# Self attention of a fused decoder layer: v as the weight in four column strips, sums taken from the exponentials, and a new order of the steps around them

## The reference, cut to what matters

```python
def _L0_attn_ref(x, Wq, Wk, Wv, Wo):            # H=32 heads, HKV=8 groups of G=4, DH=16
    q = (x @ Wq.T).reshape(b, t, H, DH).transpose(0, 2, 1, 3)
    k = (x @ Wk.T).reshape(b, t, HKV, DH).transpose(0, 2, 1, 3)
    v = (x @ Wv.T).reshape(b, t, HKV, DH).transpose(0, 2, 1, 3)
    q, k = rope(q), rope(k)
    scores = jnp.einsum('bhgtd,bhkd->bhgtk', q.reshape(b, HKV, G, t, DH), k) / math.sqrt(DH)
    scores = jnp.where(causal, scores, jnp.finfo(jnp.float32).min)
    attn = jax.nn.softmax(scores, axis=-1)
    ctx = jnp.einsum('bhgtk,bhkd->bhgtd', attn, v)
    return ctx.reshape(b, H, t, DH).transpose(0, 2, 1, 3).reshape(b, t, E) @ Wo.T

x = _layernorm(x + attn(x)); x = _layernorm(x + cross(x, ctx)); x = _layernorm(x + ffn(x))
```

## Time and profile before

| | |
|---|---|
| median of 3 runs | 1139.7 us (1138.28 to 1140.21) |
| profiled execution | 1137.65 us |
| its span, first to last instruction | 1135.9 us |
| mean granted clock of PE | 0.992 of full |
| busy: PE, PEld, DVE, ACT, POOL | 97%, 86%, 47%, 48%, 20% |
| chain that ended last | PE 90%, DVE 3%, ACT 3% |
| self attention, with the first cross projections | about 0 to 231 us of the span |
| cross attention, 16 groups | about 231 to 1076 us |

### The profile page before, as it was taken

How to read it: one execution, slowest core, us unless ns; L and a number is a source line. 1 busy time by engine, 2 the same in 40 slices (tenths; PEclk the granted TensorE clock), 3 DMA queues, 4 the chain that set the end, 5 groups by cost and what they waited for, 6 DMA issues and landing times.

```text
span 1135.9 us, 20112 instructions
## 1 busy us (share of the span) xinstructions
PE 1103.6 (97%) x6892; PEld 980.8 (86%) x6892; DVE 535.6 (47%) x2002; ACT 541.2 (48%) x1336; POOL 223.5 (20%) x235
## 2 busy tenths in 40 slices
PE   6899998999999999999999999999999999999897
PEld 5899998878888888888888888888888888888785
DVE  4577767544434343434243435344343444343584
ACT  5778776444444443444443443444444435344412
POOL 6335444321010101111010101010101011110142
PEclk9899998999999999999999999999999999999999
DMA  4401100132011010102020202021110101000001
GB/s 145 158 11 28 32 2 1 29 140 80 28 52 60 18 60 18 60 18 76 3 78 0 78 0 78 0 78 31 47 60 18 60 18 60 18 23 1 1 1 74
DMA packets 16600, 49.63 MB, mean 44 GB/s; under 512 B 2480, under 2 KB 4912, under 8 KB 16048
## 3 DMA queue, kind: packets, MB, share of 16 engines
q1 hardware_dynamic: 16272, 44.93, 11.6%
q0 software_dynamic: 288, 4.19, 0.9%
HBM read 47.02 MB, written 2.10 MB: 43 GB/s over the span
## 4 chain that ended last, share of the span: by engine, by line
PE 90%; DVE 3%; ACT 3%; issue 1%; DMA 1%; POOL 1%; SPq 0%; POOLq 0%; DVEq 0%; ACTq 0%
PE bank L650 49%; PE bank L1396 15%; PE bank L1383 5%; PE bank L1366 5%; PE bank L499 4%; PE bank L585 4%; PE bank L1414 3%; PE bank L1373 2%; PE bank L573 1%; PE bank L1320 1%; DMA v_raw<-in_wv 1%; PE bank L1452 1%; DMA stage<-in_wq 1%; DVE sm L429 1%; PE bank L509 0%
## 5 line engine op out<-in xcount | busy, mean ns | idle before, releaser
L810 POOL TENSOR_TENSOR bm<-mask,bias 128x512 f32<-128x512 f32 x64 | 96.9, 1515 | 715.6 <-DVE nmx L1090 460.9
L922 ACT ACTIVATE pr<-sm,nmx 128x128 f32<-128x128 f32 x256 | 99.8, 391 | 162.7 <-DVE nmx L1090 162.5
L1102 DVE TENSOR_TENSOR at_lo<-bank,at_hi 128x512 fp32r<-128x512 f32 x64 | 44.3, 692 | 252.8 <-ACT at_hi L936 252.8
L1108 DVE TENSOR_TENSOR acc<-acc,bank 128x512 f32<-128x512 f32 x128 | 87.8, 687 | 120.3 <-PE bank L1396 120.3
L915 ACT COPY v<-bank 128x256 f32<-128x256 f32 x124 | 46.2, 373 | 118.9 <-PE bank L650 67.7
L1396 PE MATMUL bank<-wo_hi,at_hi 128*128 128x512 f32 x256 | 101.2, 395 | 0.0
L1396 PE MATMUL bank<-wo_lo,at_hi 128*128 128x512 f32 x256 | 100.6, 393 | 0.0
L1396 PE MATMUL bank<-wo_hi,at_lo 128*128 128x512 f32 x256 | 99.9, 390 | 0.0
L650 PE MATMUL bank<-wv_hi,cT_hi 128*128 128x256 f32 x512 | 92.0, 302 | 0.0
L650 PE MATMUL bank<-wv_hi,cT_lo 128*128 128x256 f32 x512 | 81.9, 282 | 0.0
L650 PE MATMUL bank<-wv_lo,cT_hi 128*128 128x256 f32 x512 | 81.9, 282 | 0.0
(11 more groups left out here) (210 smaller groups left out, 2300.8 us busy)
## 6 DMA issues: line engine op xcount, KB each, us to landing
qk_raw<-in_wqk SPq DMA_DIRECT2D x31, 512.0 KB, 4.4
o_raw<-in_wo SPq DMA_DIRECT2D x16, 512.0 KB, 3.3
v_raw<-in_wv SPq DMA_DIRECT2D x15, 512.0 KB, 4.3
xT_raw<-in_xT SPq DMA_DIRECT2D x8, 256.0 KB, 2.7
acc<-in_x POOLq DMA_DIRECT2D x1, 2048.0 KB, 9.3
stage<-in_cT POOLq DMA_DIRECT2D x1, 2048.0 KB, 13.4
bias<-in_bias SPq DMA_DIRECT2D x16, 128.0 KB, 3.0
out<-acc SPq DMA_DIRECT2D x8, 256.0 KB, 2.0
```

The lines of the kernel that those rows point to most:

```text
L810: nc.gpsimd.tensor_tensor(bm[:, s % 2], mask[:, HALF * (s // HG):HALF * (s // HG + 1), :], bias[:, s % HG:s % HG + 1, :].broadcast_to([P, ...
L922: e = nc.scalar.activation(pr[:, s % 2, k], sm[:, s % 2, k], ACT.Exp, bias=nmx[:, s % 2, k:k + 1], accum_out=sums[:, s % 2, k:k + 1])
L1102: nc.vector.tensor_tensor(at[1][:, s // HG, s % HG], PO[:], f32(at[0][:, s // HG, s % HG]), ALU.subtract).then_inc(s_al, 1)
L1108: nc.vector.tensor_tensor(acc[:, b], acc[:, b], PX[b % 2][:], ALU.add).then_inc(s_acc, 1)
```

## The change

**v is the weight.** `pv(b, odd)` runs twice per element, for the even groups (0, 2, 4, 6) and the odd ones (1, 3, 5, 7). Its weight is 32 columns of a padded v (`v1` holds pairs of groups with zeros between them), its moving operand the 512 columns of a transposed tile of four heads, its output one of four strips of 32 partitions of one bank. The even products start the sums, the odd ones add to them. The output is already transposed, in another order of its rows; Wo is laid out in that order on the host. The tiles are worked through in the order of `GROUPS`. Five buffers (`RING`) hold transposed tiles, two of the old ones and three in `stage`.

**Sums from the exponentials.** Odd tiles sum by `accum_out` of ACT's exponentials, even tiles by a `tensor_reduce` of DVE. DVE takes one reciprocal per element, of the 32 sums widened to 512 columns. Four PE transposes (`spread`) turn it, ACT copies it to `y`, and DVE multiplies the output bank by it.

**Other moves in the self attention.** The widened copy of q goes from ACT to POOL, one step earlier; the rotation's sum and the turn of q one step earlier; the addition of x with its statistics, the layer norm's steps and the xn transposes move to other steps; the Wo product is cut in two halves (j=6 and j=7); the Wo weight is split by POOL and, in four pieces, DVE; part of the first k stack is copied by DVE; k and v of element 3 are projected at t=2, j=6.

**Between the stages.** The context comes in two halves of 1 MB: the first by POOL at t=2, j=7, the second by SP once the first is split, behind the second half of the first q and k weights, which now goes into `qk_raw[0]` once that is split. The high parts of the first cross weights are made by POOL and one element earlier. The first cross tiles have another order; one k product goes to a bank of scores (S[1]).

**Last group.** The last transposed copy (ACT) comes before the last exponentials; the first output product before the transposes of x; the low part of the last attention output before `norm_x`.

```diff
-            self.on = left(first, "on", [P, H1, DH1])
+            self.on = left(first, "on", [P, D])
-            self.v1 = left(first, "v1", [P, 4, G1, DH1 + 1])
+            self.v1 = left(first, "v1", [P, 4, G1 // 2, 3 * DH1])
...
+    GROUPS = (0, 2, 4, 6, 1, 3, 5, 7)
...
# POOL
-            if j == (3 if t == 1 else 5) and live(t):
+            if j == (3 if t == 1 else 4) and live(t):
                 ...   rot = rot_a + rot_b
+            if j == 5 and live(t):
+                nc.gpsimd.tensor_copy(q3[:, :, 0:2 * DH1]..., rot[:, 0:D]...broadcast_to([P, H1, 2, DH1])).then_inc(s_hi3, 1)
+            if j == 3 and t == 2:
+                nc.gpsimd.tensor_copy(wout[0][:], wout_raw).then_inc(s_wohi, 1)
-            if j == 6 and t == 2:
+            if j == 7 and t == 2:
                 nc.gpsimd.dma_start(acc[:], a["x"]).then_inc(s_res, 16)
-                nc.gpsimd.dma_start(stage[:], a["cT"]).then_inc(s_stage, 16)
+                nc.gpsimd.dma_start(mem.cT_raw, mem.context_half(a["cT"], 0)).then_inc(s_stage, 16)
# ACT
                     act.wait_ge(s_neg, n // 2 + 1)
+                    at_least(act, s_rs, b - 1)
                     for r in range(R1):
-                        e = nc.scalar.activation(pr[:, 1, r], sm[:, 1, r], ACT.Exp, bias=nmx[:, r:r + 1])
+                        e = nc.scalar.activation(pr[:, 1, r], sm[:, 1, r], ACT.Exp, bias=nmx[:, r:r + 1],
+                                                 accum_out=sums1[b % 2][:, GROUPS[i], r:r + 1])
...
-                at_least(act, s_pv, n - 1)
-                nc.scalar.copy(prT[:, i % 2], ...).then_inc(s_ptc, 1)
+                if n >= RING:
+                    act.wait_ge(s_pv, (n - RING) // 4 + 1)
+                nc.scalar.copy(prT[n % RING], pt_bank[i % 2][:]).then_inc(s_ptc, 1)
...
+            if j == 3 and live(t - 3):
+                b = t - 3
+                act.wait_ge(s_R, b + 1)
+                at_least(act, s_x1, b)
+                nc.scalar.copy(y[:], O1[:]).then_inc(s_Rc, 1)
# DVE
-        def normalise(b, i):
-            nc.vector.reciprocal(rs[:, hs], o[:, :, DH1]).then_inc(s_rs, 1)
-            nc.vector.tensor_tensor(on[:, hs, :], o[:, :, 0:DH1], rs[:, hs]..., ALU.mult).then_inc(s_on, 1)
-            if j == 1 and live(t - 4):
+            if j == 2 and live(t - 4):
                 ...   x1, xn
+            if j == 2 and live(t - 3):
+                b = t - 3
+                dve.wait_ge(s_p, G1 * (b + 1))
+                dve.wait_ge(s_sum, G1 // 2 * (b + 1))
+                at_least(dve, s_R, b)
+                nc.vector.reciprocal(rs, sums1[b % 2].rearrange("p g (r one) -> p r g one", one=1)
+                                     .broadcast_to([P, R1, G1, DH1])).then_inc(s_rs, 1)
+            if j == 4 and live(t - 3):
+                b = t - 3
+                dve.wait_ge(s_Rc, b + 1)
+                dve.wait_ge(s_pv, 2 * (b + 1))
+                at_least(dve, s_onlo, b)
+                nc.vector.tensor_tensor(on[:], O0[:], y[:], ALU.mult).then_inc(s_on, 1)
+            b, i, n = tile(t, j, 1)
+            if live(b) and i % 2 == 0:
+                dve.wait_ge(s_p, n + 1)
+                at_least(dve, s_rs, b - 1)
+                nc.vector.tensor_reduce(sums1[b % 2][:, GROUPS[i], :], pr[:, 0], AX_X, ALU.add).then_inc(s_sum, 1)
# PE
-        def pv(b, i, n):
-            pe.wait_ge(s_ptc, n + 1)
-            for r in range(R1):
-                ins = nc.tensor.matmul(o_bank[h // HB][:, col:col + DH1 + 1], prT[:, i % 2, r],
-                                       v1[:, b % 4, i, :], start=True, stop=True)
+        def pv(b, odd):
+            n = b * G1 + 4 * odd
+            pe.wait_ge(s_ptc, n + 4)
+            for k in range(4):
+                ins = nc.tensor.matmul(O0[4 * k * 8:4 * (k + 1) * 8, :], v1[:, b % 4, k, odd * DH1:(odd + 2) * DH1],
+                                       prT[(n + k) % RING], start=not odd, stop=bool(odd))
+            ins.then_inc(s_pv, 1)
+        def spread(b):
+            pe.wait_ge(s_rs, b + 1)
+            at_least(pe, s_Rc, b)
+            for r in range(R1):
+                ins = nc.tensor.transpose(O1[:, r * T:(r + 1) * T], rs[:, r].rearrange("p g d -> p (g d)"), ident[:])
+            ins.then_inc(s_R, 1)
-            b, i, n = tile(t, j, 3)
-            if live(b):
-                pv(b, i, n)
+            if j == 3 and live(t - 3):
+                spread(t - 3)
+                pv(t - 3, 1)
+            if j == 6 and live(t - 2):
+                pv(t - 2, 0)
# the first cross weights: DVE, t = LAST - 2, and POOL
+                    if t == LAST - 2 and j == 3:
+                        first_lo(wqk[0], qk_raw[0][:], s_wqk_h[0], s_wqk[0])
+                    if t == LAST - 2 and j == 0:
+                        first_hi(wqk[0], qk_raw[0][:], s_qk_in[0], s_wqk_h[0])
# PE, after t = LAST - 1
             step_a(LAST, 0)
             first_project_v(3)
             step_a(LAST, 1)
-            step_a(LAST, 2)
+            step_a(LAST, 3)
+            step_a(LAST, 4)
             groups(pe, step)
# last group: ACT, PE
+                    if last and s == TILES - 1:
+                        copy_prT(n - 1, False)
                     exps(n, s, first)
...
-                    transpose_x2(0)
-                    transpose_x2(1)
                     for j in range(HALF):
                         output(HALF + j, 1, n if j == 0 else None)
+                        if j == 0:
+                            transpose_x2(0)
+                            transpose_x2(1)
```

More of the change, by code:

```diff
@@ L103, in __init__ @@
         self.stage = left(whole, "stage", [P, KC * B * T])
+        self.cT_raw = self.stage[:, KC * HALF * T:2 * KC * HALF * T].rearrange("p (c n) -> p c n", c=KC)
         self.ident = left(whole, "ident", [P, P])
@@ L573, in scores, with output @@
                 ins = nc.tensor.matmul(SA[:, 2 * k * T:2 * (k + 1) * T],
-                                       q3T[b % 2][:, 2 * j + k, :], k3T[b % 2][:, j, :], start=True, stop=True)
+                                       q3T[b % 2][:, 2 * g + k, :], k3T[b % 2][:, g, :], start=True, stop=True)
             ins.then_inc(s_s, 1)
-        def pv(b, i, n):
-            pe.wait_ge(s_ptc, n + 1)
-            if i in (0, G1 // 2):
-                at_least(pe, s_on, 2 * b - 1 + 2 * i // G1)
-                pe.wait_ge(s_v1, b + 1)
-            for r in range(R1):
-                h = R1 * i + r
-                col = (h % HB) * (DH1 + 1)
-                ins = nc.tensor.matmul(o_bank[h // HB][:, col:col + DH1 + 1], prT[:, i % 2, r],
-                                       v1[:, b % 4, i, :], start=True, stop=True)
-            ins.then_inc(s_pv, 1)
+        def pv(b, odd):
+            n = b * G1 + 4 * odd
+            pe.wait_ge(s_ptc, n + 4)
+            if not odd:
+                at_least(pe, s_on, b)
+                pe.wait_ge(s_v1, b + 1)
+            for k in range(4):
[5 more added lines that the diff above has]
+            at_least(pe, s_Rc, b)
+            for r in range(R1):
+                ins = nc.tensor.transpose(O1[:, r * T:(r + 1) * T],
+                                          rs[:, r].rearrange("p g d -> p (g d)"), ident[:])
+            ins.then_inc(s_R, 1)
+        def output(b, part):
+            pairs = [(onT[p][:, c, :], wout[q][:, c, :]) for p, q in PARTS for c in range(KC)]
+            half = len(pairs) // 2
+            for i in range(part * half, (part + 1) * half):
+                ins = nc.tensor.matmul(QB[:], *pairs[i], start=i == 0, stop=i == len(pairs) - 1)
+            if part == 1:
+                ins.then_inc(s_wout, 1)
         def step(t, j):
@@ L617, in step @@
                 four(KVB, [xn[:, c * P:(c + 1) * P] for c in range(KC)]).then_inc(s_xnT, 1)
-            if j == 4 and live(t - 3):
-                pe.wait_ge(s_on, 2 * (t - 2))
-                pe.wait_ge(s_v1, min(t + 1, B))
-                at_least(pe, s_xnlo, t - 3)
-                four(KVB, [on[:, 8 * c:8 * c + 8, :].rearrange("p h d -> p (h d)") for c in range(KC)])\
-                    .then_inc(s_onT, 1)
             if j == 0 and t == 1:
@@ L630, in step @@
             if j == 6 and t == 3:
-                pe.wait_ge(s_wo1, 1)
+                pe.wait_ge(s_wo1, KC)
             if j == 6 and live(t - 3):
-                if t - 3 >= B - 2:
-                    pe.wait_ge(kT_taken, t - 3 - (B - 2) + 1)
+                if t - 3 == B - 2:
+                    pe.wait_ge(kT_taken, 1)
+                if t - 3 == B - 1:
+                    pe.wait_ge(s_y, B - 1)
                 pe.wait_ge(s_onlo, t - 2)
                 pe.wait_ge(s_rq, min(t + 1, B))
-                product(nc, QB[:], [[(onT[p][:, c, :], wout[q][:, c, :]) for c in range(KC)]
-                                    for p, q in PARTS]).then_inc(s_wout, 1)
+                output(t - 3, 0)
+            if j == 7 and live(t - 3):
+                output(t - 3, 1)
         return step
@@ L997, in step @@
                         copy_q(n + 1, s + 1)
```

(19 more changed lines are left out.)

269 lines of the change are left out of this document (139 added, 130 removed).

## The result

The changed kernel takes 1161.86 us (median of 4 runs, 1160.52 to 1164.08) against 1139.48 for the kernel before on the same chip: a ratio of 1.0206, 95% interval 1.0178 to 1.0235. It is slower by 22.4 us. The prediction had the direction and the range right, and the size wrong: +11 us was forecast, half of what came. The profiled execution took 1164.08 us, the longest of the four, with a span of 1162.3, 26.4 us more than the profiled span before.

What follows compares the result with a forecast made beforehand. PE, busy 97% of the 1135.9 us span, was taken as the bound. Terms +8, +3.5, 0, -4, +5, -2.5, -2 and +3 were summed to +11 on about 1139.7: a median of 1151 us, range 1122 to 1174.

Steps and rivals of the forecast that it cites:

- step 3: Self-attention step where PE asks for the reciprocals at 3.4 us, ready at 6.0: PE stands 2.6 us per element.
- The price of the strips: Products with v, self attention: staggered passes, four strip matmuls 2.15 us, eight 4.3 us per element, against 6.5 removed.
- the layout: Settled self-attention element laid out by hand from row prices: waits in steps 3, 5 and 6, about 26.0 us in all.
- The waits around the reciprocal: Each settled self-attention element grows between +0.4 (one wait) and +2.7 us (hand layout); +2.0 taken.
- The clock: Long PE waits invite the lower clock, each costing about 3 us; one more than now: +3, tied to no stage.
- Up to t=2: Start of the self attention: ACT's split of the output weight goes to POOL, -2.5 us.
- t=8, t=9 and the end: Late self attention and last group: +3.5 (reciprocal stays), -4 (idle and clock loss go, 1 us wait stays), -2 (reordering).
- t=4 to 7: The four settled self-attention elements: 4 x 2.0 = +8 us.
- From t=10 on: PE waits 7.3 us at the spread for inverse roots and DVE, less about 2 already in later waits: +5.
- The stage of t=3: Self-attention element at lower clock: 23.26 us now, 26 by the hand layout; 0 taken, v product moved ahead.
- Serial strips: Rival, chance 0.15: strips don't overlap, PE pays 2.6 us more per element, eight times: +20, about 1171 us.
- The faster case: Rival, chance 0.33: eight strips 1.7 us, one reciprocal wait: -19, about 1121; or reciprocal 0.7 us: 1120 to 1132.

Runs made afterwards that it cites:

- a dose: Kernel with narrow reciprocal, odd product before spread and q copy on ACT, plus its four even strip products sent twice: 1121.29 us, ratio 0.9869 to the kernel before.
- first experiment: Changed kernel, but the reciprocal is taken of the 32 sums and a DVE copy widens it to 512 columns afterwards: 1141.58 us, ratio 1.0045 to the kernel before.
- fifth experiment: First experiment plus, right behind the copy, a wide DVE reciprocal of 512 columns that nobody reads: 1154.31 us, ratio 1.0167 to the kernel before.
- third experiment: Changed kernel with the widened copy of q moved back from POOL to ACT (the third edit): 1155.28 us, ratio 1.0167 to the kernel before.
- fourth experiment: Changed kernel with three edits together: narrow reciprocal widened by a copy, odd product before the spread, q copy on ACT: 1122.48 us, ratio 0.9879 to the kernel before.
- the second: Changed kernel, but PE does the odd product with v before the spread of the reciprocals: 1150.75 us, ratio 1.0133 to the kernel before.

## Why the prediction was right or wrong

**Right: direction, place and price of the reciprocal.** The straight line through three narrow reciprocals gave 3.2 us for 512 columns, measured 3.34; the wait before the spread was put at 2.6 us in step 3, measured 2.84 in the settled elements; it stands there eight times. DVE was put at 22.6 us per element, measured 22.3. The Trainium skill's eight passes per element (VectorE: DVE Perf Modes, First, the fixed hardware budget), 4.3 us by the estimate made then, are too dear for what these rows show. The sums cost 0.68 (0.65 taken), the exponentials with sums 0.39 apart as forecast. PE's gain is even larger than thought.

**Wrong: the size,** in five steps of the sum. The price of the strips erred one way, the other four the other way. (The terms of the sum add up to +11.0, not 11.3, and the waits of the layout to 25.8 us per element, not 26.0; neither matters here.)

- *The price of the strips* ("pass 1 of the next strip goes beside pass 2 of the last": 2.15 us for four). Measured 0.99, and 0.87 as a dose. The rival's price, 1.7 for eight, was the right one (1.74 to 1.98). The Trainium skill's ratio (TensorE: Matmul & The Clock Gate, Part 3), 2.9 us for eight by the estimate made then, is nearer than mine and still too dear here. This error alone would have made the forecast too slow by 2.2 us per element. That it didn't makes the next one larger.
- *The waits around the reciprocal* ("between +0.4 and +2.7 I take +2.0"). Measured +3.47, with strips 2.2 us cheaper than in the layout: waits and half clock are 26.75 less about 19.6 of PE's work, 7.2 us, where the layout had 4.9 and I took less than it. Three things were missing from it. The two operations of the layer norm right ahead of the reciprocal take 0.54 + 1.41 us, not 1.3, since xn is made beside POOL. The ring's hold on ACT was seen, but not how long it lasts: 5.03 us. And the clock falls behind the wait, 1.33 us per element (first experiment). The layout was also walked from one place, PE before the spread; the fifth experiment shows that a wide reciprocal which nobody reads comes out at the scores and costs 3.5 us there. A loop of scores, maximum and one bank goes through DVE eight times per element. The prediction spoke of DVE's idle time as one sum ("this slack is what the change spends"), 5.9 us per element, but it lies in pieces, none longer than 1.89 us in the four settled elements. Timeline of DVE before:

```profile
104.16 0.29 DVE L429 CUSTOM_DVE_ANT_0 sm<-bank,causal 128x128 f32<-128x128 f32 x1 [1.89 <-issue]
```

That the length of the pieces decides is an argument; no run cut the reciprocal up.
- *The clock* ("one more than now: +3"). It fell to 0.50 in every settled element, each time for 3 us or more. It is no term of its own but a surcharge on each long wait: the odd strips cost 1.87 us instead of 0.99, the transposes 1.04 instead of 0.59, some 1.3 us in the element shown. Half clock does not cost that everywhere: in the first experiment's second settled element it made PE busy for 21.02 us instead of 19.85, and the element is 23.44 instead of 23.33.
- *Up to t=2* ("ACT's split of the output weight ... goes to POOL: -2.5"). Measured +7.12 at the start of t=3, 1.6 of which are there already at the first sum of the rotation, within its scatter. The split was costed, the copy of q that goes the same way was costed for its own duration only. What it does to its queue (the low part of x behind it) and to DVE's copies beside it was named for one operation (the negation, 1.47) and not for the copies of k, nor for a stretch where nothing overlaps. The third experiment takes that back, 5.2 us. The gain of 2.5 does not show even there: the stage of t=2 takes 22.43 us, against 21.89 before.
- *t=8, t=9 and the end:* +5.36 for +3.5, -2.15 for -4, -0.45 for -2. The first is the same wait, 3.83 us there instead of 2.84; in t=9 it is 3.75, where I let one microsecond stay because the first cross projections would fill it. They come behind the spread, not ahead of it. From t=10 on the forecast was close: 7.3 us of waiting, measured 8.08, and +5.57 for +5. The stage of t=3 came out 2.1 us shorter, where 0 was taken.

The sum of these misses: head +9.6, t=4 to 7 +5.0, t=8 and t=9 +3.7, the rest 0.0 (t=3 -2.1, t from 10 +0.6, the end +1.5), less the 3 for the clock that is in them: 15.4, which is 26.4 less 11.

**The rivals.** Serial strips are out. The faster case had the right strips and failed on its condition, one wait of 2.6 us and less than 2.2 us of hold on ACT. With the waits taken away by three edits (fourth experiment) the same strips gave 0.9879, that is 1125.7 us on the scale of the 1139.5 us of before; the rival said 1121, with the wide reciprocal kept.

## What to carry to other kernels

Before an engine's idle time is spent, look where it lies: when the engine is one station of a loop that runs many times per element, a single operation of 3 us stalls that loop once, even if nobody reads its result. Making it short helped most (3.4 us per element); putting work that does not need the result ahead of its reader helped too (2.0). Cutting it up was not tried. Widen after a costly elementwise operation, not before: 32 reciprocals and a copy did in 1.2 us what 512 reciprocals did in 3.3. When an operation moves to an idle engine, cost what stands behind it in that queue and what the other engine does at the same time, at the start of the kernel as well as in its settled part.

## What the runs showed of the hardware

- Four fp32 matmuls of 512 columns in four 32-column strips take 0.99 us together, and four more behind them 0.87: the price of one (0.86). I had expected two passes to get in each other's way.
- The granted clock fell to 0.50 behind each of the four settled waits of 2.84 us and behind the one of 1.97 us in the fifth experiment (the product after it took 1.20 us instead of 0.72). Behind waits of 1.84 to 1.88 us it fell twice in the settled elements of the second and fifth (at 85.06 and 88.71 us) and stayed full six times, at 109.84 and 114.53 us for example: the length of the wait alone does not tell.
- DVE's copies from SBUF to SBUF take longer beside POOL: 1.31 us instead of 0.36 for 384 columns, 0.82 instead of 0.23 for 128. The operation that makes xn took 1.41 us beside POOL, and 0.75 in an element of the kernel before.
- A reciprocal costs 0.34 us for 32 columns and 3.34 for 512: 6.2 ns per column, near the 6.0 of the small ones of the earlier trace rows.
- What stays open: why the changed kernel's last step takes 4 us more than that of the fifth experiment was read from the trace alone; whether 3.3 us on DVE cost less when cut into pieces; why the third edit shortens the settled elements; and which engine sets the element of 21.17 us in the fourth experiment.
